# A four-layer conditioned sequence kernel: the maximum of |Wh| through TensorE, a reordered head, the running sum of the batch stage in PSUM, and ScalarE emptying the result banks one step earlier

## Time and profile before

| | |
|---|---|
| timed executions | 1585.09 us median of 3, 1581.67 to 1589.25 |
| profiled execution | 1587.56 us, span in the trace 1585.7 us |
| TensorE matmul busy | 1474.3 us, 93% of the span |
| VectorE / ScalarE / GpSimd busy | 66% / 42% / 43% |
| DMA | 167.77 MB, mean 106 GB/s |
| mean granted TensorE clock | 0.956 of 2.4 GHz |

### The profile page before, as it was taken

The page is one execution under the profiler, slowest core; times in us unless marked ns, Lnnn a source line. Parts: engine busy times, 40 slices in busy tenths (PEclk is TensorE's granted clock), DMA queues, the critical chain, the costliest instruction groups (busy, mean ns, idle before and its releaser), DMA issues. The chain is left out here.

```text
span 1585.7 us, 48981 instructions
## 1 busy us (share of the span) xinstructions
PE 1474.3 (93%) x20708; PEld 1149.6 (72%) x20708; DVE 1041.3 (66%) x2722; ACT 667.3 (42%) x2182; POOL 683.9 (43%) x540
## 2 busy tenths in 40 slices
PE   4758999999999999999999999999989958999998
PEld 3435888788888878888887888888767745666666
DVE  3323566675757576666667575757566778888884
ACT  3324444544454545444454445454444312233332
POOL 2214343433444443534343344444243447565653
PEclk9779999999999999999999999999989988899999
DMA  8263042414232333424241423233244657776762
GB/s 325 90 239 137 14 66 52 75 35 89 37 74 49 62 55 61 67 51 74 43 83 32 84 42 68 49 62 50 41 102 112 123 95 252 257 274 226 263 238 82
DMA packets 443118, 167.77 MB, mean 106 GB/s; under 512 B 407906, under 2 KB 411106, under 8 KB 439571
## 3 DMA queue, kind: packets, MB, share of 16 engines
q1 hardware_dynamic: 442898, 164.64, 41.3%
HBM read 96.25 MB, written 68.16 MB: 104 GB/s over the span
## 5 line engine op out<-in xcount | busy, mean ns | idle before, releaser
L438 PEld LDWEIGHTS recb<-hs,scanS 128*128 128x128 f16 x16384 | 444.2, 96 | 179.4 <-DVE hs L1092 171.2
L438 PE MATMUL recb<-hs,scanS 128*128 128x32 f16 x16384 | 495.6, 177 | 24.5 <-DVE hs L1092 24.5
L622 ACT ACTIVATE hs<-pre 128x64 f16<-128x64 f32 x512 | 131.6, 257 | 647.9 <-DVE pre L1087 647.5
L1085 DVE TENSOR_TENSOR pre<-recb,xw 128x64 f32<-128x64 f32 x512 | 115.0, 225 | 291.8 <-PE recb L438 287.9
L956 DVE RECIPROCAL gates<-gates 128x64 f32<-128x64 f32 (+1 forms) x484 | 257.9, 554 | 0.4
L1092 DVE TENSOR_TENSOR hs<-konst,hs 128x64 f16<-128x64 f32 x512 | 114.9, 224 | 137.3 <-ACT konst L623 137.3
L819 POOL TENSOR_TENSOR xt<-xt,hbuf 128x512 f32<-128x512 f32 x64 | 98.6, 1541 | 207.3 <-ACT hbuf L626 207.3
L807 POOL TENSOR_TENSOR x1lo<-xt,x1hi 128x512 fp32r<-128x512 f32 x62 | 79.7, 1285 | 196.3 <-ACT x1hi L632 189.6
L823 POOL TENSOR_TENSOR gates<-gates 128x512 f32<-128x512 f32 x64 | 83.0, 1297 | 159.5 <-DVE gates L956 159.5
L832 POOL TENSOR_TENSOR xt<-xt,pout 128x512 f32<-128x512 f32 x64 | 75.9, 1186 | 169.8 <-DVE pout L982 169.8
L1087 DVE TENSOR_TENSOR pre<-recb,pre 128x64 f32<-128x64 f32 x512 | 114.8, 224 | 17.6
(11 more groups left out here) (197 smaller groups left out, 2867.6 us busy)
## 6 DMA issues: line engine op xcount, KB each, us to landing
xt<-in_x SPq DMA_DIRECT2D x64, 256.0 KB, 3.5
g_d<-gst SPq DMA_DIRECT2D x64, 256.0 KB, 3.8
n_d<-nst SPq DMA_DIRECT2D x64, 256.0 KB, 3.0
x_d<-xt SPq DMA_DIRECT2D x64, 256.0 KB, 3.0
out<-gates SPq DMA_DIRECT2D x64, 256.0 KB, 2.5
xt<-x_d SPq DMA_DIRECT2D x28, 512.0 KB, 5.3
stage<-in_w SPq DMA_DIRECT2D x11, 1024.0 KB, 8.9
xt<-g_d SPq DMA_DIRECT2D x14, 512.0 KB, 7.1
```

Source lines behind the costliest of these rows:

```text
L438: last = nc.tensor.matmul(rec[:, m].rearrange("p a b -> p (a b)"), w[:, k, m * P:(m + 1) * P], hs[:, k].rearrange("p a b -> p (a b)"), sta ...
L622: nc.scalar.activation(hs[:, :, 0, :], pre[t % 2][:], ACT.Tanh, scale=unscale).then_inc(s_h, 1)
L1085: nc.vector.tensor_tensor(pre0[:], rec[:, :, 0, :], xw[j % 2][:, t], ALU.add).then_inc(s_pre0, 1)
```

## The change

It has three parts; the head's buffers and semaphore counts follow from them (s_wh counts to 9 instead of 8).

1. Head: the maximum over partitions goes through TensorE (a transpose into PSUM, a reduction of one row on VectorE, the four scale values made in that row, and a matmul with a row of ones that spreads them). `partition_all_reduce` is gone. The layer norm moves behind the gate on ScalarE and VectorE; W2 is loaded ahead of cond. Wi gets a buffer of its own (`rawi`), gate weights load earlier, ScalarE and GpSimd split them earlier, `hgT` is copied a step earlier.
2. Batch stage, VectorE: from batch 1 on the sum scan of `hidden` writes to PSUM (`aux`), and the addition reads it there.
3. Batch stage, ScalarE: the four `put_out` stand ahead of `x3_high(C * b + 2)`.

```diff
-for _step, _item in ([(2 + m, ("x1h1", m)) for m in range(C)] + [(7 + n, ("w", n)) for n in range(C)] + [(13 + 4 * m + 1, ("x", m)) for m in range(C)]
-                     + [(15 + n, ("w", C + n)) for n in range(C)] + [(21 + n, ("w", 2 * C + n)) for n in range(C)]
+for _step, _item in ([(2 + m, ("x1h1", m)) for m in range(C)] + [(1 + n, ("w", n)) for n in range(C)] + [(13 + 4 * m + 1, ("x", m)) for m in range(C)]
+                     + [(7 + n, ("w", C + n)) for n in range(C)] + [(18 + n, ("w", 2 * C + n)) for n in range(C)]
...
-DVE_FIRST_LATE = {1: [("x11", 0)], 2: [("x11", 1)], 3: [("hgT",), ("x11", 2)], 4: [("x11", 3)], 15: [("x1", 0)], 18: [("x1", 1)], 21: [("x1", 2)], 24: [("x1", 3)]}
+DVE_FIRST_LATE = {1: [("x11", 0)], 2: [("hgT",), ("x11", 1)], 3: [("x11", 2)], 4: [("x11", 3)], 15: [("x1", 0)], 18: [("x1", 1)], 21: [("x1", 2)], 24: [("x1", 3)]}
...
+        peak, spread = recb[0:1, 3 * P:4 * P], recb[:, C * 2 * B:C * 2 * B + 4]
-        raw = xt[3][:]
+        raw = {"f": xt[3][:], "i": rawi[:], "c": xt[3][:]}
...
             def gate_weight(n):
-                if n:
-                    sp.wait_ge(s_w3l, C * n)
-                else:
-                    sp.wait_ge(s_wxl, C)
+                if n == 0:
+                    sp.wait_ge(s_wxl, C)
+                elif n == 1:
+                    sp.wait_ge(s_z, 4)
+                else:
+                    sp.wait_ge(s_w3l, C)
...
             gate_weight(0)
-            sp.dma_start(c2s[:], a["c2"]).then_inc(d_c2, 16)
-            unit(2)
-            sp.wait_ge(s_z, 4)
+            gate_weight(1)
             for m in range(C):
                 load_x(2, m)
+            unit(2)
+            sp.dma_start(c2s[:], a["c2"]).then_inc(d_c2, 16)
             unit(3)
             unit(4)
-            gate_weight(1)
+            gate_weight(2)
             unit(5)
             unit(6)
             factors_out(0)
-            unit(7)
-            gate_weight(2)
-            unit(8)
-            unit(9)
-            unit(10)
+            for u in range(7, 11):
+                unit(u)
...
             pe.wait_ge(d_wh, 16)
+            pe.wait_ge(s_mx, 1)
+            pe.wait_ge(s_turned, 2)
+            nc.tensor.transpose(peak, whs[:, 0:1], ident[:]).then_inc(s_amx, 1)
+            pe.wait_ge(s_ae, 1)
+            for c in range(C):
+                last = nc.tensor.transpose(cols[:, c, :], ae[:, c * P:(c + 1) * P], ident[0:B, 0:B])
+            last.then_inc(s_cols, 1)
             pe.wait_ge(s_colsT, 1)
             dense(condT, wh, None, z)
             pe.wait_ge(d_h1, 16)
             dense(aeT, w1h, 2, z3)
+            pe.wait_ge(s_wh, 5)
+            nc.tensor.matmul(spread, ones[:], whr[:, 0:4], start=True, stop=True).then_inc(s_bc, 1)
...
                 y_high(b - 1)
-                x3_high(C * b + 2)
                 for t in range(NT):
                     put_out(b - 1, t)
+                x3_high(C * b + 2)
                 x3_high(C * b + 3)
...
-            pool.wait_ge(s_mx, 1)
-            nc.gpsimd.partition_all_reduce(whs[:, 1:2], whs[:, 0:1], P, bass.bass_isa.ReduceOp.max).then_inc(s_amx, 1)
...
                 if s < 3:
-                    add_h(0, s)
                     for n in range(C * s, C * (s + 1)):
                         weight_low(n)
+                    add_h(0, s)
...
             dve.wait_ge(s_amx, 1)
-            nc.vector.tensor_scalar(whs[:, 2:3].bitcast(I32), whs[:, 1:2].bitcast(I32), 0x7F800000, None, ALU.bitwise_and).then_inc(s_wh, 1)
+            nc.vector.tensor_reduce(whr[:, 4:5], peak, axis=AX.X, op=ALU.max).then_inc(s_wh, 1)
             dve.wait_ge(s_wh, 1)
+            nc.vector.tensor_scalar(whr[:, 2:3].bitcast(I32), whr[:, 4:5].bitcast(I32), 0x7F800000, None, ALU.bitwise_and).then_inc(s_wh, 1)
...
+            dve.wait_ge(s_bc, 1)
+            nc.vector.tensor_copy(whs[:], spread).then_inc(s_wh, 1)
...
                 dve.wait_ge(s_u, k + 1)
-                nc.vector.tensor_tensor_scan(nin[b % 2][:, m, :], konst[:], nin[b % 2][:, m, :], 0.0, ALU.mult, ALU.add).then_inc(s_H, 1)
+                total = aux[:] if b else nin[0][:, m, :]
+                if b:
+                    dve.wait_ge(s_x3, k)
+                nc.vector.tensor_tensor_scan(total, konst[:], nin[b % 2][:, m, :], 0.0, ALU.mult, ALU.add).then_inc(s_H, 1)
                 loaded(dve, "x", k)
                 dve.wait_ge(s_H, k + 1)
-                nc.vector.tensor_tensor(xin[b % 2][:, m, :], xin[b % 2][:, m, :], nin[b % 2][:, m, :], ALU.add).then_inc(s_x3, 1)
+                nc.vector.tensor_tensor(xin[b % 2][:, m, :], xin[b % 2][:, m, :], total, ALU.add).then_inc(s_x3, 1)
```

More of the change, by code:

```diff
@@ L100, in build @@
         with ExitStack() as early:
+            rawi = early.enter_context(nc.sbuf_tensor("rawi", [P, C, D], F32))
+        with ExitStack() as early:
             row = early.enter_context(nc.sbuf_tensor("row", [1, 3, D], F32))
@@ L108, in build @@
         sbx, bias = bias4[:, 0, :], {k: bias4[:, n + 1, :] for n, k in enumerate("fic")}
-        whs = sb("whs", [P, 4])
+        whs, whr = sb("whs", [P, 4]), sb("whr", [1, 5])
         warm = sb("warm", [P, 1])
@@ L114, in build @@
         aeT, hT, hgT = (sb(s, [P, C, PADB]) for s in ("aeT", "hT", "hgT"))
-        stat, ones = sb("stat", [B, 4]), sb("ones", [1, PADB])
+        stat, ones = sb("stat", [B, 4]), sb("ones", [1, P])
         ae = sb("ae", [B, D])
@@ L251, in _ @@
             sp.dma_start(w1T, a["W1"]).then_inc(d_w1, 16)
-            sp.dma_start(crow, a["cond"]).then_inc(d_cond, 16)
+            sp.dma_start(w2T, a["W2"]).then_inc(d_w2, 16)
+            sp.dma_start(crow, a["cond"]).then_inc(d_ln, 16)
             for dst, k in ((lng, "ln_g"), (lnb, "ln_b")):
                 sp.dma_start(dst, a[k].rearrange("(a d) -> a d", a=1).to_broadcast([B, D])).then_inc(d_ln, 16)
-            sp.dma_start(w2T, a["W2"]).then_inc(d_w2, 16)
             for m in range(C):
@@ L493, in dense @@
                 for e in range(C if n is not None else 0):
-                    last = nc.tensor.matmul(z[e * PADB:(e + 1) * PADB, :], ones[:], row[:, n, e * P:(e + 1) * P],
+                    last = nc.tensor.matmul(z[e * PADB:(e + 1) * PADB, :], ones[:, 0:PADB], row[:, n, e * P:(e + 1) * P],
                                             start=False, stop=True, tile_position=(0, e * PADB))
@@ L513, in _ @@
             turn(sg, turned)
[L514 to L517, removed]
             for k in range(C):
@@ L538, in _ @@
             pe.wait_ge(s_sg, 3)
-            pe.wait_ge(s_wh, 8)
+            pe.wait_ge(s_wh, 9)
             pe.wait_ge(s_turned, 3)
@@ L671, in weight_high @@
                 act.wait_ge(d_raw["fic"[n // C]], 16)
-                nc.scalar.copy(split["fic"[n // C]][0][:, n % C, :], raw[:, n % C, :]).then_inc(s_w3h, 1)
+                nc.scalar.copy(split["fic"[n // C]][0][:, n % C, :], raw["fic"[n // C]][:, n % C, :]).then_inc(s_w3h, 1)
             def base_high(c):
@@ L676, in base_high @@
                 nc.scalar.copy(bhi[:, c, :], braw[:, c, :]).then_inc(s_bh, 1)
[L678 to L681, removed]
             act.wait_ge(s_z, 1)
@@ L692, in _ @@
                     nc.scalar.copy(split["x"][0][:, m + 1, :], wx[:, m + 1, :]).then_inc(s_wxh, 1)
+            act.wait_ge(s_ln, 2)
+            nc.scalar.activation(ae[:], cent[:], ACT.Square, accum_out=stat[:, 1:2]).then_inc(s_ln, 1)
+            act.wait_ge(s_ln, 4)
+            nc.scalar.activation(stat[:, 3:4], stat[:, 2:3], ACT.Sqrt).then_inc(s_ln, 1)
             act.wait_ge(s_z, 4)
@@ L1056, in _ @@
                 nc.vector.tensor_tensor(x1lo[:, m, :], xt[0][:, m, :], x1hi[:, m, :].bitcast(F32), ALU.subtract).then_inc(s_x1l, 1)
+            dve.wait_ge(s_ln, 5)
+            nc.vector.reciprocal(stat[:, 0:1], stat[:, 3:4]).then_inc(s_ln, 1)
+            dve.wait_ge(s_ln, 6)
+            nc.vector.scalar_tensor_tensor(cent[:], cent[:], stat[:, 0:1], lng, ALU.mult, ALU.mult).then_inc(s_ln, 1)
+            dve.wait_ge(s_ln, 7)
+            nc.vector.tensor_tensor(ae[:], cent[:], lnb, ALU.add).then_inc(s_ae, 1)
@@ L1061, in _ @@
             dve.wait_ge(s_wh, 2)
-            nc.vector.tensor_scalar(whs[:, 3:4], whs[:, 0:1], 2.0 ** -14, None, ALU.mult).then_inc(s_wh, 1)
-            nc.vector.tensor_scalar(whs[:, 1:2].bitcast(I32), whs[:, 0:1].bitcast(I32), -1, 254 << 23, ALU.mult, ALU.add).then_inc(s_wh, 1)
+            nc.vector.tensor_scalar(whr[:, 0:1], whr[:, 2:3], 2.0 ** -100, 2.0 ** 120, ALU.max, ALU.min).then_inc(s_wh, 1)
+            dve.wait_ge(s_wh, 3)
+            nc.vector.tensor_scalar(whr[:, 3:4], whr[:, 0:1], 2.0 ** -14, None, ALU.mult)
```

45 lines of the change are left out of this document (19 added, 26 removed).

## The result

The changed kernel takes **1518.09 us** in the median of four executions (1514.28 to 1521.22), the kernel before 1587.17 (1581.67 to 1590.3, four) beside it: a ratio of **0.9567**, 95% interval 0.953 to 0.9604. The forecast was 1520.5 us, with a range of 1508 to 1544.

A forecast was written before the change was run, and what follows sets the result against it. Batches were taken to be bound by a chain through ScalarE, VectorE and TensorE, closed by ScalarE's order. Savings of 39.9 (batches), 6.4 (head) and 18.3 (block 0) sum to 64.6 us: 1585.1 becomes 1520.5, range 1508 to 1544.

The forecast's parts named there:

- Part 3: Batch stage, put_out first: no bank wait left, TensorE's own period 14.07 us; alone it would stop at VectorE's 16.4.
- Part 2: Batch stage, VectorE: addition 0.69 us instead of 1.45 median, scan into PSUM 0.02 us dearer, loop 14.2 us.
- the upper bound of 0.49: VectorE's sum scan: 0.49 us extra if the write to PSUM were added whole.
- Batch stage: Fifteen periods of 14.2 us, the first 2.2 longer: 215.2 us against 255.1, 39.9 less.
- Head: Before the first sum: GpSimd's x1_low runs earlier, first sum at 40.4 instead of 46.78, 6.4 us less (4 to 9).
- Everything up to TensorE's dense(wh) moves by 2.45 us: Head: an earlier sigmoid and no wait for cond bring this stretch's end from 29.80 to 27.35.
- Block 0: Both TensorE waits for w2 pieces go (15.1 us), lower clock 1.7, hgT 1.53: 18.3 us less (12 to 20).
- the one for the lower clock: Block 0: the two late w2 pieces and few matmuls behind them no longer run at lower clock, 1.7 us.
- The low clock at each batch's start: Rival, batch stage: clock stays low there, period 15.8 us, kernel 1544; one batch in three, 1528; chance 0.17 together.
- Feeding: Rival, batch stage: waits for loaded chunks hold VectorE or GpSimd, period about 15.3 us, kernel 1537; chance 0.08.
- the 342 GB/s "at most": Batch stage, DMA: highest rate, taken from 250 GB/s at a 0.73 share, so 4.29 MB need 12.5 us.
- The scan's price of three microseconds: Slower rival, VectorE's batch loop: scan into PSUM 3.0 us instead of 1.2, loop 21.4, kernel 1626; chance 0.02.

The follow-up runs named there:

- the pair of parts: Kernel before with the change's batch-stage edits on VectorE and ScalarE and the old head: 1546.99 us, ratio 0.9742.
- the second profile: The unaltered changed kernel executed again beside later variants, as their measure: 1514.41 us, ratio 0.9557 to the kernel before.
- the kernel with the all-reduce: Changed kernel with the maximum taken by GpSimd's partition_all_reduce again, all else kept: 1521.68 us, ratio 0.9591.
- the kernel with block 0 alone: Kernel before with block 0's load order, Wi's own buffer and earlier gate weights and hgT, old head and batches: 1572.18 us, ratio 0.9901.
- the two with fills: Changed kernel with one 128x128 or three 128x40 VectorE fills per chunk of batches 1 to 15: 1517.63 and 1520.84 us.
- the kernel with part 3 alone: Kernel before with only the four put_out moved ahead of x3_high(4b + 2): 1573.08 us, ratio 0.9917.
- the three fills: Changed kernel with three 128x40 VectorE fills in each chunk of batches 1 to 15: 1520.84 us, ratio 0.9577.
- the kernel with part 2 alone: Kernel before with only the sum scan written to PSUM and the addition reading it there: 1583.97 us, ratio 0.9978.

## Why the prediction was right

The total, 1518.09 against 1520.5, is nearer than its terms. Between the two profiles 70.1 us went and not 64.6: 1.8 more in the batches, 1.3 in the head, 2.5 in block 0, all to one side. The kernel before, timed beside the changed one, lay 2.1 us above the median that the forecast started from, which hid part of that.

*Part 3.* Right: bank 0 is free before TensorE wants it, and no wait for put_out is left. TensorE's own period was put at 14.07; the pair of parts shows 14.09. Right too that alone it would stop at VectorE's 16.4 (16.55).

*Part 2.* Right: the addition at 0.69 us, the scan into PSUM 1.207 us against 1.191 in the median before, so 0.016 against the 0.02 taken and far from the upper bound of 0.49. VectorE's loop was put at 14.2 and is 14.15. The rule of VectorE: DVE Perf Modes in the Trainium skill (section "The TRN2 errata"), 62 cycles more for a source in PSUM, is not borne out by this instruction: 689 ns with one operand in PSUM against 692 at least with two in SBUF.

*Batch stage.* 41.7 us against 39.9. The first period was put at 16.4 and took 15.71, and the others 14.12 instead of 14.2. The first is in part a matter of the execution: in the second profile it took 14.16.

*Head.* 7.7 against 6.4. The step that was mis-sized is "Everything up to TensorE's dense(wh) moves by 2.45 us". The sigmoid moved by 3.6 (12.77 to 9.16), because W1's product also began earlier, at 6.58 instead of 7.98. But the first product with Wx moved by 2.58 only (19.45 to 16.87), behind ScalarE's cast, which here waited for the load of Wx. The other 1.0 came in the eight groups of products themselves, 9.37 us instead of 10.35; why is open. So the transposes, which I added behind 27.35, began at 26.24, dense(wh) at 27.18, and wh_hi, forecast at 31.4, at 30.03. Of these 1.4 us 0.5 were lost again: I had ScalarE start 0.45 us after the copy of zs begins, and behind the scaling of the bias it was 0.96 (33.62 to 34.58). ScalarE's four products took 4.21, not 4.62. TensorE's way of taking the maximum gains nothing for the scale, as the kernel with the all-reduce shows; that the scale came 1.3 us earlier than before (31.31 to 30.03) is the work of the reordering. And 6.9 of the 7.7 us hang on x1_low no longer standing behind the all-reduce.

*Block 0.* 20.8 against 18.3, just over my upper bound of 20. Both waits went and hgT's too. The term that was too small is the one for the lower clock, 1.7 us. The three steps with the waits gave back 2.1 on top of the 16.6 waited. Step 9, from its sum to the next with a piece of w2 in it, took 2.68 us instead of 3.97, and steps 5 and 27 gave 0.6 each, all at a lower clock before and at 1.00 after; step 7 went the other way, 0.6. For these I had nothing. Step 9 is a matter of the execution: the kernel with block 0 alone didn't gain it (4.14), nor did the two with fills, whose head and block 0 are those of the change.

*The rivals.* The low clock at each batch's start did not come, though the experiments show when it does: behind gaps of 1.24 us it fell in five of twelve batches, behind the four of 0.80 to 0.86 us in the kernel with part 3 alone not once, and behind the 0.3 us of the three fills not either (1.00 in the windows behind 1413.70 and 1428.20). By TensorE: Matmul & The Clock Gate in the Trainium skill (section "A second HAM failure mode: psum-queue depth-cycling"), the repeated idling between groups would have brought it down again and again. The kernel before agrees, with 0.50 to 0.54 in the 3 us behind twelve of its fourteen gaps of 1.29 to 2.19 us; with the gaps gone or at 0.3 us, no run here does. Feeding did not bound either, at a DMA share of 0.79 and 275 GB/s over the stage; the 342 GB/s "at most" was no limit, for at the first batch's start it was 402 at a share of 1.03. The scan's price of three microseconds is excluded by its row.

## What to carry to other kernels

When a chain goes round through several engines, size each engine's own loop before removing a wait: each of two edits was worth 13 us or less here, because the other's loop stood just behind, and the pair was worth 41. GpSimd's `partition_all_reduce` should be charged with the 6 to 7 us of idle time on either side of it, not with its own 0.38 us, and what stands behind it in GpSimd's program with both. And where an edit is worth less than the spread of executions, its stretch of the trace can judge it and the total can't.

## What had not been expected of the hardware

**Two rates in the middle.** A block of 32 steps takes 73.39 or 72.96 us, in executions of the same or of other kernels, and keeps its rate over hundreds of steps: all blocks from the third on in the execution with the all-reduce, and in that of part 3 alone, at 72.96; all at 73.39 in both profiles of the changed kernel; one block at 72.97 and then 73.39 in that of block 0 alone. Over thirteen blocks it is 5.6 us, more than several of the edits tried here. TensorE is busy all the time and the granted clock reads 1.00 in both. From first sum to first sum the steps differ in pattern: at 73.39 every step inside a block takes 2.292 to 2.294 us, at 72.96 steps of 2.263 and 2.297 us alternate. The kernel with block 0 alone alternates in its second and third block and stops with the fourth, where the rate changes. The small matmuls of a block take the same 26.05 or 26.06 us in both, from start to start, so the difference lies among the large ones between them. That speaks for a pattern that one step hands to the next, and against a slower clock. What starts or ends it was not found.

**The clock behind a gap is not the same each time.** In the first batch of the changed kernel it fell to 0.70 behind 1.31 us of idle time in one profile and stayed at 1.00 behind 0.67 us in the other, with 15.71 and 14.16 us for the batch; in the kernel with part 2 alone twelve batches have the same gap of 1.24 us, and in seven of them the clock stays at 1.00 behind it and the batch takes 15.6 us, while in five it falls and the batch takes over 17. Its timeline of TensorE in a batch of 15.61 us, to be read against the row at 1426.31 above, which stands in one of 17.18:

```profile
1393.52 0.50 PE L604 MATMUL bank<-wx_hi,wi_hi 128*128 128x512 f32 x1 [1.24 <-ACT gates L770]
```

The two rows are alike, and the clock isn't: 1.00 in the three microseconds behind the one, 0.55 behind the other.
